# Reordering three pieces of a fused attention and feed-forward kernel: query stack transfers, a weight sum, a projection

## What is computed

```python
x = x + L0_xattn(layernorm(x), ctx, mask)     # attention over the context itself, one head
x = x + L0_ffn(layernorm(x), w1, w2, w3)      # inputs rounded to 8-bit integers, weights to -1, 0, 1
x = x + L1_xattn(layernorm(x), ctx, mask, Wq, bq, Wk, bk, Wv, bv, Wo, bo, ...)   # 16 heads of 32
x = x + L1_ffn(layernorm(x), wq_gate, s_gate, wq_up, s_up, wq_down, s_down)      # integer weights
```

## Time and profile before

| what | us |
|---|---|
| time, median of 3 runs | 491.72 |
| lowest and highest run | 491.05, 494.46 |
| profiled execution | 492.99 |
| its span (first to last instruction) | 491.3 |
| TensorE busy in the span | 468.5 (95%) |

### The profile page before, as it was taken

One profiled execution on the slowest core, in us unless ns is written; L12 is line 12 of the kernel. 1 busy time (PEld: TensorE's weight loads), 2 busy tenths in 40 slices (PEclk: granted clock), 3 DMA queues, 4 the chain that ended last, 5 costly groups with the idle time before them and its releaser, 6 DMA issues.

```text
span 491.3 us, 10113 instructions
## 1 busy us (share of the span) xinstructions
PE 468.5 (95%) x3951; PEld 355.9 (72%) x3951; DVE 294.6 (60%) x557; ACT 235.4 (48%) x362; POOL 84.5 (17%) x105
## 2 busy tenths in 40 slices
PE   8999999999989999999999669799989999999997
PEld 6877788778757566776788558688876665556996
DVE  4964464458846987655765233778885986555111
ACT  4655433554376365554746546767654482222000
POOL 2210400014024000000162011223332143000000
PEclk9999999999998999999999988999999999999999
DMA  8999797823495336333387985977314452000111
GB/s 276 335 347 361 279 291 228 318 80 130 115 346 149 81 79 159 89 87 75 90 302 212 271 239 179 336 240 238 111 48 128 126 159 80 1 0 0 39 56 56
DMA packets 59181, 82.75 MB, mean 168 GB/s; under 512 B 20097, under 2 KB 43649, under 8 KB 57985
## 3 DMA queue, kind: packets, MB, share of 16 engines
q1 hardware_dynamic: 59136, 82.14, 53.2%
q10 hardware_dynamic: 2, 0.01, 0.0%
HBM read 58.76 MB, written 14.42 MB: 149 GB/s over the span
## 4 chain that ended last, share of the span: by engine, by line
PE 82%; DVE 10%; issue 3%; DMA 3%; ACT 1%; SPq 0%; POOL 0%; DVEq 0%; ACTq 0%
PE psum L1534 14%; PE psum L187 11%; PE psum L189 11%; PE psum L1584 7%; PE psum L1376 5%; PE psum L652 4%; PE psum L1443 4%; PE psum L1490 4%; PE psum L1321 4%; PE psum L1473 3%; PE psum L1385 3%; PE psum L1493 3%; PE psum L1338 3%; DMA xres<-x 2%; PE psum L1502 2%
## 5 line engine op out<-in xcount | busy, mean ns | idle before, releaser
L189 PE MATMUL psum<-wv_p,kv_p 128*128 128x512 f32 x288 | 76.2, 413 | 0.0
L187 PE MATMUL psum<-kv_p,wk_p 128*128 128x384 f32 x384 | 75.5, 347 | 0.0
L187 PEld LDWEIGHTS psum<-kv_p,wk_p 128*128 128x128 f32 x384 | 67.9, 191 | 2.1 <-issue 0.2
L189 PEld LDWEIGHTS psum<-wv_p,kv_p 128*128 128x128 f32 x288 | 53.7, 188 | 15.8 <-issue 3.9
L1201 ACT ACTIVATE e<-psum,mask_bias 128x448 f32<-128x448 f32 x96 | 53.9, 634 | 22.5 <-PE psum L1473 22.3
L1490 PE MATMUL psum<-e,vst 128*32 128x112 f32 x768 | 38.0, 269 | 3.8 <-issue 2.0
L1868 DVE TENSOR_SCALAR e<-e 128x1344 f32<-128x1344 f32 x32 | 29.1, 910 | 19.9 <-ACT e L1201 19.9
L1534 PE MATMUL psum<-xt,wg_b 128*128 128x448 f16 x176 | 36.9, 353 | 0.0
L1534 PE MATMUL psum<-xt,wu_b 128*128 128x448 f16 x176 | 36.9, 352 | 0.0
L1584 PE MATMUL psum<-h_p,wd_r 128*128 x176 | 36.7, 369 | 0.0
L209 DVE SCALAR_TENSOR_TENSOR khl<-psum,bqk,khl 128x384 f16<-128x384 f32 x32 | 19.6, 613 | 27.8 <-ACT khl L199 27.7
(11 more groups left out here) (188 smaller groups left out, 821.4 us busy)
## 6 DMA issues: line engine op xcount, KB each, us to landing
kst<-k_scratch SPq DMA_DIRECT2D x32, 384.0 KB, 6.3
kv_raw<-in_ctx_feat SPq DMA_DIRECT2D x12, 768.0 KB, 5.3
w_stage<-in_w SPq DMA_DIRECT2D x6, 1408.0 KB, 9.4
cn<-in_ctx_tok SPq DMA_DIRECT2D x8, 768.0 KB, 9.8
k_scratch<-khl SPq DMA_DIRECT2D x128, 48.0 KB, 1.7
v_scratch<-vsp SPq DMA_DIRECT2D x24, 256.0 KB, 2.7
vst<-v_scratch SPq DMA_DIRECT2D x8, 768.0 KB, 4.7
qst<-qhl SPq DMA_DIRECT2D x32, 112.0 KB, 4.5
```

What stands on the lines that cost most here:

```text
L187: mm = pe.matmul(psum[:, kv_bank(p), 0:TP], wk_p[:, u, k, n * P:(n + 1) * P], src[:, v, k, :], **ends)
L189: mm = pe.matmul(psum[:, kv_bank(p), :], src[:, u, k, n * P:(n + 1) * P], wv_p[:, v, k, :], **ends)
```

## The change

The sixteen stack DMAs of the second half are no longer issued eight and eight, but two behind each of the eight key fetches of b = 0 and b = 1. The sum of w3 over partitions moves on TensorE from before key piece 35 to behind it and the gate chunk `gate_up(1, 1, 0)`; VectorE's `mean_weight` moves into `third_input`, and GpSimd's `rms(0, 0)` ahead of the scaling of w3. The projection of tile 4 moves ahead of the last values.

```diff
-        def queries_stack(sp, n, pair):
+        def queries_stack(sp, n, pair, parts):
             gs_of = slice(2 * pair, 2 * pair + 2)
             sp.wait_ge(q_lo, G * n + 2 * pair + 2)
-            for u in range(2):
-                for hh in range(4):
-                    sp.dma_start(qst[n][64 * u:64 * u + 64, hh, gs_of]...
+            for u, hh in parts:
+                sp.dma_start(qst[n][64 * u:64 * u + 64, hh, gs_of]...
+
+        STACK_PARTS = [(u, hh) for u in range(2) for hh in range(4)]
...
-            queries_stack(sp, 0, 0)
-            queries_stack(sp, 0, 1)
+            queries_stack(sp, 0, 0, STACK_PARTS)
+            queries_stack(sp, 0, 1, STACK_PARTS)
             values_fetch(sp, 0, 0)
             values_fetch(sp, 1, 1)
-            queries_stack(sp, 1, 0)
             for b in range(B):
                 for g in range(G if b + 2 < B else 0):
                     sp.wait_ge(s_sum, TC * (G * b + g + 1))
                     keys_fetch(sp, b + 2, g)
-                if b == 0:
-                    queries_stack(sp, 1, 1)
+                    if b < 2:
+                        queries_stack(sp, 1, b, STACK_PARTS[2 * g:2 * g + 2])
...
+            rms(0, 0)
             scale_weight(pool, 2, 0)
-            rms(0, 0)
             scale_weight(pool, 2, 1)
...
             gate_up(0, 0, 2)
+            keys_values((35,))
+            gate_up(1, 1, 0)
             for p in range(A_PIECES - 2, A_PIECES):
                 kv_wait_read(pe, p)
             total_weight(pe, 2, B_DN)
-            keys_values((35,))
-            gate_up(1, 1, 0)
             keys_values((36,))
...
                     if g == 0 and 1 <= b < 4:
                         spread(b - 1)
+                    if (b, g) == (B - 1, G - 1):
+                        project(pe, 4)
                     values(b, g)
             normalized_turn(pe, 3)
             spread(B - 1)
-            project(pe, 4)
...
             def third_input():
                 keys_values((35,))
                 input_integers(dve, 2)
+                mean_weight(dve, 2, B_DN)
 
-            mean_weight(dve, 2, B_DN)
             row_scale(0, 0, third_input)
```

More of the change, by code:

```diff
@@ L532, in build @@
         ALL_PARTS = parts_until(TILES - 1)
-        def queries_stack(sp, n, pair):
+        def queries_stack(sp, n, pair, parts):
             gs_of = slice(2 * pair, 2 * pair + 2)
             sp.wait_ge(q_lo, G * n + 2 * pair + 2)
-            for u in range(2):
-                for hh in range(4):
-                    sp.dma_start(qst[n][64 * u:64 * u + 64, hh, gs_of].rearrange("p g s -> p (g s)"),
-                                 qhl[n][32 * hh:32 * hh + 32, :, gs_of].rearrange("d v g s -> d v (g s)")).then_inc(q_stacked[n][pair], 16)
+            for u, hh in parts:
+                sp.dma_start(qst[n][64 * u:64 * u + 64, hh, gs_of].rearrange("p g s -> p (g s)"),
+                             qhl[n][32 * hh:32 * hh + 32, :, gs_of].rearrange("d v g s -> d v (g s)")).then_inc(q_stacked[n][pair], 16)
+        STACK_PARTS = [(u, hh) for u in range(2) for hh in range(4)]
         e = [at(f"e{r}", [P, TC, 4 * S], F32, 56576 + r * 5376) for r in range(4)]
```

## The result

The changed kernel is slower. Its median is 499.56 us (499.41 to 500.24, 4 runs) against 492.49 for the kernel before in the same comparison (491.05 to 494.46); the ratio is 1.0144, with a 95% interval of 1.0104 to 1.0183. That is 7.1 us more, where 2.8 less were forecast, and it lies outside the stated range. The profiled execution took 500.24 us, with a span of 498.5.

What follows compares the result with a forecast made beforehand. TensorE was taken as the bound, busy 468.5 of 491.3 us and stopped where instruction packets wait behind queued data. Stacks -2.0, sum of w3 -0.1, projection -0.7: -2.8 us, from 491.72 to 488.9 us; range 484.0 to 494.0.

Steps and rivals of the forecast that it cites:

- third stop: TensorE's 4.39 us wait for instructions at 288.06 in the attention; to fall to about 1 us, -3.4 us.
- half clock: TensorE's 1.2 GHz stretch from 292.98 to 299.50, behind the 4.39 us stop; to go, -2.5 us.
- first two stops: TensorE's instruction waits at 273.43 (1.78 us) and 279.72 (2.61 us); to stay, within 1 us either way.
- stop after (1,3): New wait for the first later instruction packet, behind stacks queued with the keys of b = 1: +1.5 us, bounds 0 to 3.5.
- later stops: Packet due after (2,1), behind value fetch 3 and Wo: +2.4 us, bounds 0 and 6; the last two stops stay.
- Per group SP issues 2.1 us: One key fetch and two stacks need 2.15 us of DMA time, so the queue stays about 3 us deep from 283 to 295.
- The next packets: TensorE's instruction packets in the attention from about 282.3 on, to cause waits of about 1, 1.5 and 2.4 us.
- second rival: Packet after (2,1) waits behind value fetch 3, Wo and keys: 6 us stop, 2.5 us slow clock; 495.0 us, chance 0.15.
- third rival: The stacks' order doesn't matter, attention stops and slow clock stay: -0.8 us in all, 490.9 us, chance 0.20.
- its halves are wanted at 158.2 and 163.1, so this is covered: Ahead of `down(0)`: GpSimd scales w3 later, from about 154.4 to 159.7, at no cost; covered by 1 us for the first half.
- The slow clock, kept out of the sum: TensorE's clock may drop at `down(0)` after two idle stops close together: about 1.6 us more, chance 4 in 10.

Runs made afterwards that it cites:

- a_stacks: The kernel before with only the change's stack order (both eights woven in twos into the key fetches of b = 0 and 1): 496.86 against 490.83 us, ratio 1.0109.
- k1: The kernel before with the first eight stacks woven in twos into the keys of b = 0, the second eight left in one block behind them: ratio 1.0019.
- k2: The kernel before with the second eight stacks woven in twos into the keys of b = 1, the first eight left where they were: ratio 1.0136.
- m2: The kernel before with the second eight stacks woven into the keys of b = 1, four behind every second key fetch: ratio 1.0086.
- j_late: The kernel before with the second eight stacks in one block behind the keys of b = 1 instead of b = 0: ratio 0.9980.
- k3: The kernel before with the first eight stacks in a block behind the keys of b = 0, the second eight behind those of b = 1: ratio 0.9973.
- b_sum: The kernel before with only the change's three moves around the sum of w3: ratio 1.0066, 3.2 us slower.
- b3_sum_early_mean: The kernel before with the sum of w3 moved, VectorE's mean ahead of key piece 35, and GpSimd's old order kept: ratio 1.0033 (0.9992 to 1.0075).

## Why the prediction was wrong, point by point

**What bounds.** Right in kind: TensorE stops where its packet of instructions is late behind data. Taking out sixteen stacks took 6.6 us off, and issuing them on another queue changed nothing. But I read one trace as if its stops were fixed. The second trace has the same sum within 2.3 us, spread otherwise: the third stop, whose 4.39 us with the clock behind it were the whole gain of my sum, is 1.41 there.

**The stacks: -2.0 forecast, +5.3 measured (3.6 to 7.1).** Term by term, in the traces of the kernel before and the changed one, with 2.5 us for each stretch of half clock as in the prediction:

| term | forecast, us | measured, us |
|---|---|---|
| first two stops | 0 | +0.4 |
| third stop | -3.4 | -2.6 |
| half clock | -2.5 | +2.5 |
| stop after (1,3) | +1.5 | +5.2 |
| later stops | +2.4 | -0.6 |
| sum | -2.0 | +4.9 |

The step that failed is the price of the transfers, and with it the depth of the queue.

- "Per group SP issues 2.1 us and the DMA engines need 1.05 + 2 x 0.55 = 2.15 us." The price of a key fetch was taken from stretches in which keys ran almost alone. Woven at b = 1, a group needs 3.0 us (at b = 0, at 236 GB/s from 276 to 285, about 2.6), so eight groups need some 5 to 7 us more DMA time than my sum had. SP issues a group in 2.1 us, and the queue gets deeper all the while instead of standing still: the key fetches of b = 1 land 7.0 to 11.8 us after their issue. The queue was to run dry near 281 to 282; the DMA engines stay full to 285.
- "Up to there the same bytes are queued as before, so the first two stops (1.8 and 2.6) stay". Neither stayed within 1 us: the first shrank to 0.24, the second became 4.53 (4.81 in `a_stacks`). Their sum hardly moved, 4.8 us against 4.4, so little was lost here; `k1`, woven at b = 0 alone, has one of 3.95 and costs nothing that is told.
- The next packets: forecast 1, 1.5 and 2.4 us, measured 1.81 for the one that I put at 1, and 5.20 for the one after (1,3), with a slow clock behind it. The size and the slow clock look like my second rival (6 + 2.5 us), to which I gave 0.15, but that rival had them one packet later, with value fetch 3, Wo and the keys of b = 2 ahead. Here value fetch 3 was issued at 300.33, when the stop began (300.57), and a key fetch issued at 293.46 was still on its way until 305.3: what was ahead was mostly the woven backlog of b = 1. `k2` and `m2`, woven only there, have the same stop (4.93), the blocks of `j_late` and `k3` do not. So the nearness to the rival's price is luck; no rival of mine had this mechanism. The third rival, that the stacks don't matter, is out: their order alone costs 5.3 us.
- The slow clock was to go (-2.5). It doubled. One stretch now follows the second stop, as it does in the second trace of the kernel before (there behind 2.89 us), and one the new stop of 5.20.

**The sum of w3: -0.1 forecast, +3.2 measured (1.6 to 4.9).** That TensorE's 1.75 us would come back as idle time before `down(0)` was right in kind: 4.6 us of it, forecast 3.8. That VectorE's chain decides was right too. What failed is "its halves are wanted at 158.2 and 163.1, so this is covered". The halves were ready in time; the cost is that GpSimd's second scaling now runs while VectorE rounds the first half, which takes 1.92 us longer (3.53 against 1.61); some 0.6 of these come from the scaling's own lengthening beside line 1736. I had looked at when results are due, and not at who runs beside whom. The slow clock, kept out of the sum at 4 in 10 and 1.6 us, came in `b_sum` (1.7 us, from 97.7 to 99.4) and is absent from that column in the changed kernel, where the clock fell ahead of `down(0)` instead, hidden by the wait for VectorE. What else `b3_sum_early_mean` may still lose, 1.6 us with an interval that holds 0, stays open.

**The projection: -0.7 forecast, -0.8 (+0.8 to -2.4) measured.** The ratio alone tells nothing here. In two traces the time behind the (7,2) values fell from 7.3 to 6.8 us, with the idle time filled as forecast; I had 6.6.

## What to carry to other kernels

A price for a transfer holds beside the traffic in which it was read: a burst of one kind may be cheap and the same bytes woven into another kind dear. Try kinds in blocks first (here they were never slower than woven), and look at GB/s at full share, not at the share alone. When an operation of GpSimd is moved, list VectorE's operations in its new time and not only the times at which results are due. Where stops come from a shared resource that is near full, take two or three traces before building on the size of one.

## What the runs showed of the hardware that I had not expected

- Key fetches out of DRAM and stack transfers within SBUF, alternating, move 202 to 221 GB/s with the DMA engines full (`k2`), against 330 and more (keys, nearly alone) and 185 (stacks) in blocks (`j_late`). The key packets take 241 to 251 ns instead of 123 to 158.
- A large VectorE operation from SBUF to SBUF that starts beside GpSimd's scaling ends only after it: 3.53 instead of 1.61 us on line 340, 1.68 instead of 0.54 on line 489. It works the other way too: a scaling that met a VectorE operation took 3.28 instead of 2.64 us. A VectorE operation on one column (0.21 us) and one that reads PSUM (0.74 us) were not slowed.
- TensorE's packets of instructions are late for data on any queue: with the stacks on GpSimd's queue the sum of the stops was 7.7 us, not much under the 9.1 and 11.4 of the kernel before, and the time the same (1.0019, 0.9990 to 1.0047).
- TensorE went on 1.2 to 1.7 us after the packet of instructions had landed, at all but one of the "issue" stops of 0.5 us or more. The profile puts some stops of this kind down to another engine (1.58 us at 337.46 in the changed kernel, to ScalarE), so the sum under "issue" can be too small.
